# A graph convolution with residual and layer norm on one core: kept blocks chosen in pairs, first copies of x split over two engines, last row block normalised on VectorE

## What is computed

```python
A = adj + eye(8192)
deg = A.sum(axis=1)
d = rsqrt(deg)
A_hat = A * d[:, None] * d[None, :]
h = (A_hat @ x) @ w
y = x + elu(h)
out = (y - y.mean(-1)) / sqrt(y.var(-1) + 1e-5)
```

## Time and profile before

| | us |
|---|---|
| median of 3 runs | 1069.43 (1068.69 to 1070.45) |
| the profiled execution | 1070.84 |
| its span in the trace | 1069.0 |
| PE busy | 926.4 (87%) |
| DVE busy | 784.5 (73%) |
| ACT busy | 701.7 (66%) |
| POOL busy | 199.1 (19%) |
| moved by DMA | 369.67 MB |

### The profile page before, as it was taken

The page is one execution under the profiler, slowest core; times in us unless marked ns, Lnnn a source line. Parts: engine busy times, 40 slices in busy tenths (PEclk is TensorE's granted clock), DMA queues, the critical chain, the costliest instruction groups (busy, mean ns, idle before and its releaser), DMA issues.

```text
span 1069.0 us, 36263 instructions
## 1 busy us (share of the span) xinstructions
PE 926.4 (87%) x16384; PEld 860.0 (80%) x16384; DVE 784.5 (73%) x661; ACT 701.7 (66%) x1689; POOL 199.1 (19%) x268
## 2 busy tenths in 40 slices
PE   0089299499498998989999999999999999999994
PEld 0087289498498997989999999879799998989994
DVE  0586587666767786868867899899888876867933
ACT  6888889888888898988988888830264627200202
POOL 0210120300403103041241344573111000000000
PEclk9999789799699999999999999999999999999997
DMA  9999999999999999999999999979798989899920
GB/s 379 397 394 406 394 396 404 393 401 398 395 395 389 396 379 398 381 394 387 397 391 400 390 382 364 345 248 372 248 287 288 312 266 317 252 311 310 365 89 21
DMA packets 171915, 369.67 MB, mean 346 GB/s; under 512 B 6256, under 2 KB 33520, under 8 KB 164080
## 3 DMA queue, kind: packets, MB, share of 16 engines
q1 hardware_dynamic: 154864, 358.96, 91.4%
q10 hardware_dynamic: 16896, 8.39, 2.7%
HBM read 363.13 MB, written 4.19 MB: 344 GB/s over the span
## 4 chain that ended last, share of the span: by engine, by line
PE 47%; issue 29%; DVE 7%; DMA 7%; POOL 7%; ACT 2%; SPq 1%; POOLq 0%; DVEq 0%; ACTq 0%
PE p_set L872 45%; DMA space<-in_adj 7%; POOL space L761 4%; DVE space L890 3%; DVE space L903 2%; PE p_set L850 2%; ACT space L778 1%; DVE hT L914 1%; SPq L723 1%; POOL xn L754 1%; POOL space L742 1%; POOL d L748 1%; ACT space L809 0%; DVE stats L943 0%; DVE space L937 0%
## 5 line engine op out<-in xcount | busy, mean ns | idle before, releaser
L872 PE MATMUL p_set<-space 32*128 32x256 f32 (+2 forms) x16256 | 908.8, 381 | 128.6 <-DVE space L903 60.3
L872 PEld LDWEIGHTS p_set<-space 32*128 32x128 f32 x16256 | 843.7, 187 | 189.6 <-issue 138.7
L890 DVE STREAM_TRANSPOSE space<-space 128x2048 f32<-128x2048 f32 x256 | 580.7, 2293 | 125.5 <-ACT space L778 94.0
L778 ACT ACTIVATE space<-space 128x512 f32<-128x512 f32 (+2 forms) x756 | 581.8, 770 | 99.0 <-DMA space<-in_adj 90.8
L914 DVE TENSOR_TENSOR hT<-p_set,hT 128x1024 f32<-128x1024 f32 (+1 forms) x107 | 105.0, 997 | 91.8 <-PE p_set L872 91.3
L778 ACT ACTIVATION_READ_ACCUMULATOR space<-space 128x1 f32 x756 | 141.0, 187 | 0.0
L801 ACT ACTIVATE space<-space 128x512 f32<-128x512 f32 x16 | 10.1, 630 | 191.5 <-DVE space L925 191.4
L761 POOL COPY space<-xn 32x512 f32<-32x512 f32 x192 | 123.3, 642 | 11.9
L748 POOL TENSOR_TENSOR d<-deg,half 128x4 f32<-128x4 f32 x16 | 16.3, 1019 | 538.2 <-DVE deg L896 538.1
L786 ACT ACTIVATE space<-xn 32x512 f32<-32x512 f32 x80 | 50.2, 627 | 40.6 <-POOL xn L754 34.9
L768 POOL TENSOR_TENSOR rstd<-var_eps,half 128x4 f32<-128x4 f32 x16 | 16.5, 1032 | 278.9 <-DVE var_eps L952 278.9
(11 more groups left out here) (15 smaller groups left out, 27.5 us busy)
## 6 DMA issues: line engine op xcount, KB each, us to landing
space<-in_adj SPq DMA_DIRECT2D x337, 1024.0 KB, 13.7
xn<-in_x SPq DMA_DIRECT2D x21, 256.0 KB, 12.3
space<-in_x ACTq DMA_DIRECT2D x16, 256.0 KB, 7.8
out_rows<-space ACTq DMA_DIRECT2D x16, 256.0 KB, 8.8
w_sb<-in_w SPq DMA_DIRECT2D x1, 64.0 KB, 1.8
```

Source lines behind the costliest of these rows:

```text
L778: ins = nc.scalar.activation(view[:, g], view[:, g], ACT.Copy, accum_out=to[:, g:g + 1])
L872: ins = nc.tensor.matmul(to, xs_chunk(h, j)[quadrant(q)], moving, start=first and s == b == 0, stop=last and s == b == 3)
L890: nc.vector.transpose(slots[slot], slots[slot]).then_inc(tile_turned, 1)
```

## The change

- `kept_units` goes through the row blocks of a band two at a time, (r, r+1) with r even, from the diagonal upwards, and keeps both or neither. `KEEP` becomes (12, 10, 8) and `FEED` 12. Now 54 tiles are kept and 82 come again. For bands 0 to 7 the kept tiles are the same; for bands 8 to 15 the number of tiles that are multiplied in the first pass (kept ones and firsts) changes from 11, 11, 8, 6, 6, 6, 4, 3 to 10, 10, 10, 8, 4, 4, 4, 4.
- `FIRST_COPIES`: of the four s = 0 chunks DVE now makes two and ACT two. The list of `plan` gives them rank 0 on both.
- `allowed`: once every part has been given out, the product with `w` need not wait for the previous one to be scaled.
- The last row block is normalised by DVE (four `tensor_scalar`) with a semaphore of its own; ACT still stores it.

```diff
-KEEP = (12, 9, 7)
+KEEP = (12, 10, 8)
-FEED = 10
+FEED = 12
-FIRST_COPIES = [("dve", [(0, q) for q in range(Q)]), ("pool", [(s, q) for s in (1, 2, 3) for q in range(Q)])]
+FIRST_COPIES = [("dve", [(0, 0), (0, 1)]), ("act", [(0, 2), (0, 3)]), ("pool", [(s, q) for s in (1, 2, 3) for q in range(Q)])]
...
-    for t, r in sorted(((t, r) for t in range(BANDS) for r in range(t + 1)), key=lambda v: (v[0], -v[1])):
-        if all(alive[m] < (KEEP[0] if m < KEEP[1] else KEEP[2]) for m in range(r, t + 1)):
-            kept.add((t, r))
-            for m in range(r, t + 1):
-                alive[m] += 1
+    for t in range(BANDS):
+        for r in range(t // 2 * 2, -2, -2):
+            rows = [u for u in (r, r + 1) if u <= t]
+            spans = [sum(u <= m for u in rows) for m in range(t + 1)]
+            if all(alive[m] + spans[m] <= (KEEP[0] if m < KEEP[1] else KEEP[2]) for m in range(r, t + 1)):
+                for u in rows:
+                    kept.add((t, u))
+                for m in range(r, t + 1):
+                    alive[m] += spans[m]
...
-            return free_set() is not None and counts["residuals"] > 0 and counts["outs"] == counts["z"]
+            return free_set() is not None and counts["residuals"] > 0 and (counts["outs"] == counts["z"] or not parts_left())
...
+    def parts_left():
+        return sum(len(p[2]) for p in parts) < BANDS * BANDS
...
-            offer("act", 1, "normalise", arg, 1.7)
+            offer(*(("act", 1, "normalise", arg, 1.7) if arg < BANDS - 1 else ("dve", 1, "normalise", arg, 1.6)))
...
-                act.wait_ge(normed, n + 1)
+                if n < BANDS - 1:
+                    act.wait_ge(normed, n + 1)
+                else:
+                    act.wait_ge(last_normed, 1)
...
+                elif kind == "normalise":
+                    n = arg
+                    dve.wait_ge(shift_ready, n + 1)
+                    for b in range(BLOCKS):
+                        ins = nc.vector.tensor_scalar(pos[:, n % RING, b], pos[:, n % RING, b], rstd[:, n % RING, b:b + 1],
+                                                      shift[:, n % RING, b:b + 1], ALU.mult, ALU.add)
+                    ins.then_inc(last_normed, 1)
```

More of the change, by code:

```diff
@@ L627, in gcn_resnorm @@
         normed = sem("normed")
+        last_normed = sem("last_normed")
         stored = [sem(f"stored{n}") for n in range(RING)]
```

## The result

| | before | after |
|---|---|---|
| median of 20 runs, us | 1069.39 | 1065.6 (1063.42 to 1068.66) |
| median span of these runs | 1067.8 | 1063.5 |
| ratio, 95% interval | | 0.9968 (0.9959 to 0.9977) |
| the profiled execution: time, span | 1070.84, 1069.0 | 1068.32, 1066.5 |

The changed kernel is 3.8 us faster. 1064.8 was forecast, and 1059.8 to 1070.0 as the range. All medians are of fast runs: two runs of one variant, with the end undone, took 1324.66 and 1737.93 us at a mean granted clock of 0.75 and 0.57 and are left out.

The account below looks back on a forecast made before the run. Transfers bind the kernel first, then PE from band 9's start at 591.25. Terms +3.45 - 4.4 - 3 + 0.9 + 1 - 2.6 = -4.65 us on 1069.43 give 1064.8; 8-in-10 range 1059.8 to 1070.0.

Parts of the forecast that it names:

- 126 tiles, no single ones: From band 9's start on PE: 126 tiles left instead of 125, +3.45 us; no single-tile parts, -4.4 us.
- Small waits, -3: PE from band 9's start to the last add: half of 6.7 us of small waits goes, -3 (0 to -6.7).
- Clock, +1: PE after idling ahead of band 9: the granted clock drops and costs +1 us (0 to 2).
- Gate of band 9, +0.9: Start of band 9 on PE: ACT's copies end later, so it opens at 592.1 instead of 591.25, +0.9 (-1.4 to +3.6).
- swallowed by the next gate: PE's low clock after idling ahead of bands 7 and 8: hidden by the following band's wait, so no cost at the end.
- So no gain ahead of a gate passes through it: Starts of bands: set by transfer queue positions, so PE arriving earlier only waits longer; no size given.
- gates at other times than before in bands 1 to 9: Sign of being wrong: if bands 1 to 9 opened at changed times, the transfer queue count would be worth nothing.
- Copies, cost nothing to ACT: ACT's 32 first copies, 20 us, are hidden in over 90 us of its waiting for transfers ahead of sums.
- gates slip: Rival, chance 0.12: ACT's copies one tile sum (2.71 us) late at band 9 or 10, making 1072.5 us.
- Tail, -2.6: After the last add: last product sent at once, -1.44, and DVE normalising the last row; -2.6 in all (-1.4 to -3).
- The prediction's side sentence: DVE normalising the last row: two elements a cycle would make the four instructions 0.27 us shorter; not in the sum.

Follow-up runs that it names:

- first profile: The changed kernel as measured against the kernel before, its profiled execution: 1068.32 us, span 1066.5; the median of its 20 runs is 1065.6 us.
- second profile: The changed kernel, nothing altered, run and profiled once more: 1066.03 us, ratio 0.9956 to the kernel before, profile span 1063.9 us.
- the runs with pairs that have them too (15 and 3.1 us): Kernel before with only the kept tiles in pairs and FEED 12, 1083.95 us; changed kernel with FEED back at 10, 1069.63 us.

## Why the prediction came out right, step by step

The time was off by 0.8 us, but of its terms only some held, and two errors cancel: the gate of band 9 came later than forecast, and the idle time behind it fell by more. That the sum came so close is luck. The reckoning "start of band 9, then 3.45 us per tile and 18.2 us of products" gives 452.9 us for what follows the gate. The rest up to the last add is 2.5 us in the first profile of the changed kernel (1051.30 - 595.92 - 452.9) and 2.6 in the second.

- **126 tiles, no single ones: right.** No matmul of 32x128 is left, and 452.9 plus 2.5 us fits both profiles, with other starts. This was the firmest part.
- **Small waits, -3: right in its sign, too small.** They were 6.7 us, and half was taken. PE's idle time behind the start of band 9 fell from 6.9 to 0.3 us, so nearly all of it went. (The two figures of before, 6.7 and 6.9, are not the same thing: 2.45 us of idle time lie among the two single tiles side by side, at 899.69 and 905.62, and are in the -4.4.) With the old kept tiles and all else changed, 8.5 us of it are back, and the time is 4.8 us higher (PE has no wait at band 9 there, which gives part of it back): idle times come with the jagged pattern, as the step said, but the runs with pairs that have them too (15 and 3.1 us) show that an even pattern isn't enough.
- **Clock, +1: too small.** What remains of the 2.5 us lies behind the wait at band 9. From 596 to 600 the first profile has 48 matmuls where 80 fit, about 1.6 us; the second has 34 and 68 from its start to 600, about 1.8 us in all. Taken together, the two terms were -2 and measured 2.5 - 6.7 = -4.2.
- **Gate of band 9, +0.9: the step that missed.** It came out at +1.9 (593.11) and +4.7 (595.92) against 591.25. In the second profile ACT's queue was the bound, as the step said, with the copies at 591.57 instead of 591.2 and PE's start 1.0 us behind the 592.1 that the step gave after its discount of 0.3. In the first, DVE's queue was the bound. The step never looked up what stands ahead of the *row sum* in DVE's list. The prediction names that case for the copies of band 8 ("behind an add that waits for PE") and calls the idle time there "swallowed by the next gate". It is not swallowed: band 9's row sum stands behind an add of band 8, so PE's lateness passes through the gate where it is large enough, as in the first profile. With DVE's items moved away, ACT's copies were the bound again, and the start of 592.54 stood where the step had put it.
- **"So no gain ahead of a gate passes through it": half right.** Gains don't. Losses do: the run with all chunks on DVE starts 3 us late at band 5 and 9 us late at band 9, since late slots delay the transfers. The positions in the transfer queue give a gate's time only when nothing on DVE or ACT holds it up. One of the prediction's signs of being wrong, gates at other times than before in bands 1 to 9, came in part: POOL's scaling of x starts within 1.6 us of before at bands 1 to 7, but at 550.41 instead of 547.80 at band 8 and at 591.04 instead of 586.19 at band 9 (549.81 and 587.39 in the second profile). With DVE's row sums first it is 586.20 again at band 9.
- **Copies, cost nothing to ACT: right.** ACT's busy time rose by 10 us, and no wait of PE between band 10 and the second pass came with it. The rival "gates slip" names ACT's queue, which did hold band 9 in the second profile, but without being a tile late; its 1072.5 did not come.
- **Tail, -2.6: measured -1.9.** The product took what was foreseen (z at 1055.17, with no wait for PE). DVE's normalisation took 1.12 us for four instead of 0.88. The last store starts 12.2 us behind the last add (1063.50) instead of 14.4, and from it to the end are 3.0 us instead of 2.75. In the median spans even less came, 0.9 to 1.2.
- **Sum.** Against the first profile: +4.7 + 3.45 - 4.4 - 4.2 - 1.9 = -2.4, and the spans differ by 2.5. Against the second: +1.9 + 3.45 - 4.4 - 4.1 - 1.9 = -5.1, and the spans differ by 5.1. The medians of the spans differ by 4.3, those of the times by 3.8. The sums must close but for rounding, since the -4.2 and -4.1 are what the reckoning leaves over; measured by themselves are the start of band 9, the last add and the end.

The theory that stands at the end: the change pays because its plan leaves PE without idle time from band 9 to the end, and it pays less than it could because the work that opens a band stands in queues, on DVE behind adds that wait for PE, on ACT behind sums. The first half is seen in the traces (6.9 us against 0.3); that it is the pairs that do it is only in part shown, since each run without one part has a plan of its own. The second is carried by the two runs with gate work first: moving DVE's alone gained nothing in the median, moving DVE's and ACT's 2.9 us. What the planner would have made of each part alone can't be read from the parts: alone they cost 14 and 18 us or gain 1.2.

Open is why the new plans of the two parts alone are as bad as they are. One wait of each was found and one undone, 4 of the 18 us.

## What to carry to other kernels

- Before costing a step that opens the next stage, list what stands ahead of *each* of its links (sum, scale, copy) on its own engine. An item that waits for the engine the stage is for makes a loop: that engine's lateness comes back to it. Put such links first, on all engines of the gate: here DVE's alone gained nothing, since ACT's copies then held the gate.
- If a program makes the order from a table of durations, test a part of a change in a fixed order. New plans for one part alone cost 14 and 18 us here, more than any part is worth.
- Read two profiles before explaining 3 us. Here a drop of the clock during one band made that difference.

## What the runs showed of the hardware

After a wait of PE of 2.76 us the granted clock fell to 0.50 in one execution and stayed at 1.00 in the other, at the same place of the same program. After 2.63 us it stayed at 1.00, after 2.75 us it was at 0.62 (596.00 to 600.00). After 5.15 to 6.29 us it was at 0.50 to 0.57 just behind the wait each time (band 7 of four profiles: after waits of 5.51, 5.15, 5.31 and 6.29 us). Where it fell it cost up to 3 us (band 8: 37.87 us against 34.82), as much as the wait itself. So a shorter wait can gain more than its length: with 0.61 us of waiting ahead of band 8, in the run with DVE's gate work first, the clock stayed at 1.00 and the band took 34.82 us. And an earlier arrival of PE at a gate that another engine holds gains nothing (5.81 us of waiting at band 9, then clock 0.50).

DVE's tensor_scalar of 128x128 fp32 with two scalars per partition took 341 to 346 ns each, against 276 for bn_stats of the same width. The Trainium skill (VectorE: DVE Perf Modes, "Mode 2x_2P") gives such an instruction two elements a cycle. The prediction's side sentence made of it an estimate of 0.27 us less for the four than at one element a cycle. The trace shows no such gain, the four came out 0.24 us dearer than the four bn_stats; but no run has the form at one element a cycle, so which mode ran is not shown.
